# DLRM tower: quarters of a tile through all stages, row scaling moved from VectorE to GpSimd

## The reference

```python
x = layer_norm(dense_t @ Wd.T, gd, bd)                        # 128 wide
y = layer_norm(einsum('bnd,ed->bne', sparse_t, Ws), gs, bs)   # 26 rows x 128
y = layer_norm(einsum('bne,pn->bep', y, Wsi), gsi, bsi)       # 128 x 32
T = concatenate([x[:, None, :], swapaxes(y, 1, 2)], axis=1)   # 33 x 128
Zflat = einsum('bnd,bmd->bnm', T, T)[:, TRIL_I, TRIL_J]       # 528
z = layer_norm(Zflat @ Wl.T, gl, bl)[:, :384]                 # 512, 384 used
h = relu(concatenate([z, r_dense_t], axis=1) @ W_top1 + b_top1)
h = relu(h @ W_top2 + b_top2)
out = h @ W_top3
```

## Time and profile before

| | us |
|---|---|
| median of three runs | 779.56 (778.5 to 780.78) |
| the profiled execution | 779.52 |
| its span, first to last instruction | 777.7 |
| PE matmul busy | 582.8 (75%) |
| DVE busy | 487.4 (63%) |
| POOL busy | 455.2 (59%) |
| ACT busy | 294.0 (38%) |
| mean granted TensorE clock | 0.871 of 2.4 GHz |

### The profile page before, as it was taken

The page is one execution under the profiler, slowest core; times in us unless marked ns, Lnnn a source line. Parts: engine busy times, 40 slices in busy tenths (PEclk is TensorE's granted clock), DMA queues, the critical chain, the costliest instruction groups (busy, mean ns, idle before and its releaser), DMA issues.

```text
span 777.7 us, 18327 instructions
## 1 busy us (share of the span) xinstructions
PE 582.8 (75%) x6783; PEld 476.5 (61%) x6783; DVE 487.4 (63%) x773; ACT 294.0 (38%) x711; POOL 455.2 (59%) x628
## 2 busy tenths in 40 slices
PE   4447556869786987778778888678788887879767
PEld 3334344867675775657667676566667675758555
DVE  4628556559583958467574867458485867768810
ACT  1305533235353534243353334235353434344512
POOL 5666666666666666666666666666666666660000
PEclk9669787779899899998798899879899899999989
DMA  8200011020200202020210202121110202020110
GB/s 305 104 20 21 21 50 38 22 67 21 68 20 22 68 20 67 22 67 22 64 24 22 66 20 67 24 63 25 51 37 22 67 22 67 22 66 6 47 48 1
DMA packets 27200, 36.49 MB, mean 47 GB/s; under 512 B 8917, under 2 KB 17775, under 8 KB 26607
## 3 DMA queue, kind: packets, MB, share of 16 engines
q1 hardware_dynamic: 13808, 21.65, 7.9%
q0 software_dynamic: 13312, 13.66, 7.8%
HBM read 26.09 MB, written 9.18 MB: 45 GB/s over the span
## 4 chain that ended last, share of the span: by engine, by line
POOL 47%; issue 42%; PE 6%; POOLq 1%; DMA 1%; DVE 1%; ACT 1%; SPq 0%; DVEq 0%; ACTq 0%
POOL rows L574 41%; POOL ids L570 6%; PE bank_d L745 2%; PE bank_z L694 1%; PE bank_z L681 1%; POOLq L572 1%; PE bank_z L756 0%; POOLq L573 0%; PE bank_d L716 0%; DMA zx<-zs 0%; DVE y_var L410 0%; DMA rows<-in_table,ids 0%; PE bank_z L763 0%; PE bank_a L716 0%; DMA row_base<-in_row_base 0%
## 5 line engine op out<-in xcount | busy, mean ns | idle before, releaser
L574 POOL DMA_INDIRECT rows<-in_table,ids x416 | 407.0, 978 | 237.7 <-issue 198.8
L681 PE MATMUL bank_z<-r_vec 128*32 128x35 f32 x4096 | 77.6, 204 | 48.1 <-issue 47.3
L681 PEld LDWEIGHTS bank_z<-r_vec 128*32 128x32 f32 x4096 | 58.3, 112 | 71.7 <-issue 67.3
L896 ACT ACTIVATE y_sq<-y 128x512 f32<-128x512 f32 x128 | 75.3, 626 | 66.5 <-DVE y L400 55.8
L379 DVE COPY zs<-bank_z 128x280 f32<-128x280 f32 x32 | 14.4, 450 | 126.2 <-PE bank_z L681 65.9
L694 PE MATMUL bank_z<-wl,zd 128*128 128x512 f32 x160 | 83.2, 639 | 8.4 <-DMA zd<-zx 8.4
L424 DVE TENSOR_TENSOR r_vec<-y,y_r 128x512 f32<-128x512 f32 x128 | 83.3, 692 | 2.2
L912 ACT CAST mixed<-bank_d 64x512 fp32r<-64x512 f32 x64 | 37.1, 580 | 124.4 <-PE bank_d L716 66.0
L729 PE MATMUL bank_b<-mixed,proj_hi 128*128 128x512 f32 x64 | 36.5, 570 | 61.8 <-DVE mixed L388 59.9
L410 DVE TENSOR_REDUCE y_var<-y_sq 128x32 f32<-128x1024 f32 x64 | 77.4, 1210 | 0.7 <-ACT y_sq L896 0.7
L912 ACT CAST mixed<-bank_a 64x512 fp32r<-64x512 f32 x64 | 37.1, 579 | 75.5 <-PE bank_a L716 55.0
(11 more groups left out here) (114 smaller groups left out, 1012.7 us busy)
## 6 DMA issues: line engine op xcount, KB each, us to landing
zx<-zs SPq DMA_DIRECT2D x16, 560.0 KB
rows<-in_table,ids POOLq DMA_INDIRECT x416
dense_t<-in_dense_t SPq DMA_DIRECT2D x1, 2048.0 KB
wl<-in_wl SPq DMA_DIRECT2D x1, 1280.0 KB
w<-in_w SPq DMA_DIRECT2D x1, 1280.0 KB
zd<-zx SPq DMA_DIRECT2D x16, 80.0 KB
wsi_b<-in_wsi_b SPq DMA_DIRECT2D x1, 1248.0 KB
zd<-zx SPq DMA_DIRECT2D x16, 70.0 KB
```

Source lines behind the costliest of these rows:

```text
L574: nc.gpsimd.indirect_dma_start(rows[par][:, c, D * blk:D * (blk + 1)], None, io["table"], bass.IndirectOffsetOnAxis(ap=ids[par][:, n:n + 1 ...
L681: mm = pe.matmul(bank_z[PROJ * s:PROJ * (s + 1), j, n * ITEMS:(n + 1) * ITEMS], own[:, Y0:PAD], own, start=True, stop=True)
L896: nc.scalar.activation(y_sq[:, j % 2, blk, :], y[:, Y_PART[j], blk, :], ACT.Square)\
```

## The change

- The loops over tiles are gone. Every engine's program is written out as 64 quarters k = 4t + q, in stages w = 0 to 73. In one stage the program treats quarter w up to the row factor, quarter w-2 from `mix` to `y_scale`, quarter w-3 in `interact` and `keep_z`; the steps of `linear` and the top layers of older tiles are spread over stages. The steps before `mix` run per quarter; the chunks are grouped 4, 3, 3, 3, so that a quarter's mix needs no later chunk.
- `mix`, `turn`/`gram_product` and `interact` have one PSUM bank each now, `project` two as before. `keep_z` is all on ACT.
- Pool adds all row numbers in one instruction before the first gather. It then issues, for m = 0 to 428, `scale_half(m - 13)` and gather m. `scale_half` multiplies one half chunk (128 by 64) by its factor; this replaces `scale_rows` on DVE. At the first half chunk of each quarter it waits for `rstd_done`, the quarter's row factors.
- Before a gather of tile 2 or later Pool waits for `rows_scaled` of the same half chunk two tiles before.

```diff
-GROUPS = [range(c, min(c + 4, CHUNKS)) for c in range(0, CHUNKS, 4)]
+GROUPS = [range(0, 4), range(4, 7), range(7, 10), range(10, 13)]
+SCALE_LAG = CHUNKS
 # vector
+            for w in range(STAGES):
+                tile, q = divmod(w, BANKS)
+                new, mid = w < QUARTERS, 2 <= w < QUARTERS + 2
+                if new:
+                    square_form(w)
+                    row_mean_square(w)
+                if mid:
+                    keep_low(w - 2, 0)
+                    keep_low(w - 2, 1)
+                if new:
+                    row_reciprocal(w)
+                if mid:
+                    keep_y(w - 2, 0)
+                    keep_y(w - 2, 1)
...
+                if mid:
+                    y_mean_square(w - 2)
+                if q == 0 and 2 <= tile <= TILES + 1:
+                    linear_reciprocal(tile - 2)
+                if mid:
+                    y_reciprocal(w - 2)
+                    y_scale(w - 2, 0)
+                    y_scale(w - 2, 1)
 # gpsimd
+            def scale_half(m):
+                t, n = divmod(m, 2 * CHUNKS)
+                c, blk = divmod(n, 2)
+                q = group_of(c)
+                if n == 2 * GROUPS[q][0]:
+                    pool.wait_ge(rstd_done, BANKS * t + q + 1)
+                    if t:
+                        pool.wait_ge(mix_done, min(BANKS * (t - 1) + q + 2, BANKS * t))
+                half = slice(D * blk, D * (blk + 1))
+                nc.gpsimd.tensor_scalar(scaled[:, c, half], rows[t % 2][:, c, half], row_r[:, n:n + 1], None, ALU.mult)\
+                    .then_inc(rows_scaled, 1)
...
+            for m in range(ROWS_PER_LANE + SCALE_LAG):
+                if m >= SCALE_LAG:
+                    scale_half(m - SCALE_LAG)
+                if m < ROWS_PER_LANE:
...
+                    if t >= 2:
+                        if n == 2 * GROUPS[q][0]:
+                            pool.wait_ge(gathered[t % 2][q], (t // 2) * (32 * len(GROUPS[q])))
+                        pool.wait_ge(rows_scaled, m - 2 * (2 * CHUNKS) + 1)
                     nc.gpsimd.indirect_dma_start(
 # tensor
+            def interact(k):
+                t, q = divmod(k, BANKS)
+                if q == 0:
+                    pe.wait_ge(x_placed, t + 1)
+                if k:
+                    pe.wait_ge(zs_kept, k)
+                pe.wait_ge(r_ready, k + 1)
...
+            for w in range(STAGES + 2):
+                tile, q = divmod(w, BANKS)
+                new, mid, old = w < QUARTERS, 2 <= w < QUARTERS + 2, 3 <= w < QUARTERS + 3
+                if new:
+                    turn(w)
+                if mid:
+                    mix(w - 2)
+                if old:
+                    interact(w - 3)
+                if new:
+                    gram_product(w)
...
+                if 2 <= tile <= TILES + 1 and q == 0:
+                    linear(tile - 2, range(0, STEPS))
+                if mid:
+                    project(w - 2)
```

More of the change, by code:

```diff
@@ L86, in block_rows, with group_of @@
     return PLACES[k][0], PROJ - PLACES[k][1]
+def group_of(c):
+    return next(g for g, chunks in enumerate(GROUPS) if c in chunks)
 WINDOWS, WIN_COLS = chunk_windows()
@@ L225, in tower @@
         stored = sem("stored")
[L227 to L236 removed]
+        bank_y = [bank_b, bank_c]
+        bank_m = bank_a
+        bank_x = [bank_a, bank_d]
+        bank_t = bank_g = bank_z[:, 0, :]
+        bank_i = bank_z[:, 1, :]
+        bank_w = bank_z[:, 2, :]
+        bank_l = bank_z[:, 3, :]
         zx = nc.dram_tensor("zx", (QUAD, PROJ, BLOCKS, QUADS, STEPS), F32, kind="Internal").ap()
@@ new lines, in linear @@
+            def linear(t, steps):
+                if steps[0] == 0:
+                    pe.wait_ge(z_moved, Z_MOVES * (t + 1))
+                    pe.wait_ge(sumx_placed, t + 1)
+                    if t:
+                        pe.wait_ge(z_kept, t)
+                    else:
+                        pe.wait_ge(wl_centred, 1)
+                for s in steps:
+                    mm = pe.matmul(bank_l, zd[:, :, s], wl[:, s, :], start=(s == 0), stop=(s == STEPS - 1))
+                if steps[-1] == STEPS - 1:
+                    mm.then_inc(l_done, 1)
@@ L792, in tile_work @@
-                if top:
-                    first_layer(3)
-                if load:
-                    project(0)
-                if inter:
-                    interact(2)
-                if load:
-                    mix(1)
-                if load and not inter:
-                    fold(range(3, STEPS))
-                if load:
-                    mix(2)
-                if inter:
-                    interact(3)
-                if load:
-                    project(1)
-                    mix(3)
@@ L825, in tile_work @@
-                if more:
-                    turn(t + 1, 1 - par, 2)
-                if load and not inter:
-                    add_up_x(3)
-                if inter:
-                    linear(range(3, STEPS))
-                if more:
-                    turn(t + 1, 1 - par, 3)
-                if inter and not top:
-                    fold_bl()
-                if top:
-                    second_layer()
-                if more:
-                    gram_product(t + 1, 0)
-                    gram_product(t + 1, 1)
```

773 lines of the change are left out of this document (303 added, 470 removed).

## The result

| | before | after |
|---|---|---|
| median of three runs | 779.56 (778.5 to 780.78) | 821.53 (816.28 to 821.88) |
| ratio | | 1.052 [1.045, 1.059] |
| profiled execution, its span | 779.52, 777.7 | 821.88, 819.9 |
| POOL busy | 455.2 (59%) | 643.9 (79%) |
| granted TensorE clock | 0.871 | 0.848 |

The account below looks back on a forecast made before the run. It took Pool as the bound before and DVE and PE taking turns as the bound after: 70 + 46 x 10.75 + 15 x 13.3 - 2 + 47.6 = 810, with 44 for the clock and 1.8 outside the span 856 us (765 to 935).

Parts of the forecast that it names:

- What bounds the kernel before: Kernel before: Pool is bound by its own sequence, 43.6 us a tile; DVE and PE, 63% and 75% busy, have slack.
- Part 1: Pool's sequence after the change: a scaling and gather take 1.57 us (1.46 to 2.1), 40.8 us a tile.
- The gap of 0.81: Pool's idle time behind an addition, 0.81 us; forecast to become 0.30 behind a scaling, with 0.81 kept as the other end.
- the second rival: Pool: a scaling costs as much as an addition did, 2.08 us a pair, 940 us in all; chance 0.10.
- the rival of 0.06: DVE and Pool block one another: each y_scale half waits for a scaling, cycle gains 38 us, 894 us; chance 0.06.
- Part 2: DVE and PE take turns in each stage: 10.75 us, 13.3 with q = 0, 45.6 us a tile, bounding the kernel.
- The first rival: Pool stays the bound and the change is faster: interact's gaps don't appear, stage 9.5 us, 735 us; chance 0.14.
- Part 3: PE's clock: idle times put 40% of certain steps at the lower level, adding 44 us of a possible 110.
- Part 4: Start and end: about 70 us to the first interact, 47.6 at the end; time behind the last gather falls about 14.
- those named as wrong: Profile signs against the forecast: Pool without waits (pair above 1.85 us or stages below 10.2), interact at 1 us, square_form before interact.
- those named as right: Profile signs for it: chain with much DVE, ACT, PE; Pool waiting 2 to 8 us a tile; clock below 0.871.
- the forecast's formula for a Pool-bound kernel: Start, Pool pairs, end and time outside the span: 38.4 + 403 x 1.57 + some 62 + 1.8 gives 735 us.

Follow-up runs that it names:

- experiment 6: Kernel before with one 26-column Pool addition a tile instead of 13 two-column ones, run where the kernel before takes 797.0 to 799.5 us: 1166.83 us, ratio 1.464; again 1.457.
- Experiment 4: Changed kernel with the row scaling back on DVE at the end of each stage, Pool only gathering: 778.62 us, ratio 1.000.
- experiment 3: Changed kernel with y_scale reading its first operand from PSUM instead of the SBUF copy, leaving the bias out: 788.05 us, ratio 1.010.
- 4 (repeated): Changed kernel with row scaling back on DVE, run again where the kernel before takes 797.0 to 799.5 us: 983.2 us, ratio 1.220.
- 5: Changed kernel with row scaling back on DVE and gram_product before interact, where the kernel before takes 797.0 to 799.5 us: 1065.36 us, ratio 1.332; again 1.330.
- 7: Changed kernel without any edit, run where the kernel before takes 797.0 to 799.5 us: 862.27 us, ratio 1.081.

## Why the prediction was right, and where it was not

- **What bounds the kernel before: read from its trace, not tested; its reserve was read wrong.** The one edit of the kernel before, experiment 6, ran in the 798 condition only and made it slower. Experiment 4 takes all scalings and additions in the loop off Pool and reaches the time of before, not more. In the new order the next bound, 43.4 us a tile, lies at Pool's old 43.6.
- **Part 1, Pool's pair: the failed step.** Forecast 1.57 (1.46 to 2.1) and 40.8 a tile, measured 1.67 undisturbed and 1.78 in the mean, 46.3 a tile. Terms: the scaling 0.46, not 0.3 (between the bounds, but I leaned to the 128x2 row, where even one column takes 0.31); the gather 1.01, not 0.96; the gap 0.17, not 0.30. The gap of 0.81 did not stay, so the second rival, a scaling as dear as an addition, is out.
- **Collisions: the rival of 0.06 was real.** Its size, 38 us, was near the 33 that experiment 3 gives back. What I had wrong is who pays: `y_scale` stays at a median of 691 ns, and Pool's gathers and scalings are stretched. My evidence against it was DVE's duration beside gathers, the wrong engine to look at: the row that told it was Pool's addition of 2.02 us.
- **Part 2, the cycle: mechanism shown, one term wrong, and not the bound.** DVE waits for gram behind interact, as forecast (180.6 us in after, 100.7 in experiment 4). The wrong term is interact: 2.0, read from the earlier trace rows, and 0.7 to 0.8 measured. With 0.76 the forecast's own sum is 12.06 + 3 x 9.51 = 40.6 us, and 4 x 0.72 for its clock term makes 43.5; experiment 4 shows 43.4. By quarter the fit is looser: 12.8 against 11.93 measured with q = 0, and 10.2 against 10.24 to 10.72 for the others. The row was no odd one: from its first pass to the end of its last, an interact of before has a median of 1.85 us, and 50 of the 64 have gaps. Wrong was to carry the gaps over to the new program. The first rival named exactly this ("interact's gaps don't appear"), and gave it 0.14 only.
- **Part 3, the clock.** 44 us for 61 stages is 0.72 a stage; it was part of the sum just made and wasn't measured apart. The mean granted clock is 0.848, below 0.871 as forecast; it isn't on the path of after, where Pool sets the pace.
- **Part 4, both ends: right.** First scaling at 39.70 (38.4), Pool idle 18.64 (16), 15 us gained behind the last gather (14), 62.4 us from the end of the last gather to the end of the span (some 62 in the first rival).
- **The signs.** Two of those named as wrong came true: interact below 1 us, and Pool nearly without waits (though its pair was 1.78, not above 1.85, and no quarter's mean was below 10.2). Of those named as right, the chain with much DVE and PE and Pool's waits of 2 to 8 us a tile were absent. Stages of 10.4 to 13.2, a wait of DVE for gram of 180.6/63 = 2.9 us a stage and a clock of 0.848 came, and decided nothing: under a Pool-bound pace, quarters of 8 and 6 gathers make unequal stages too.

With the measured terms the forecast's formula for a Pool-bound kernel gives 39.7 + 403 x 1.78 + 62.4 + 2.0 = 821 us, against 821.9 for the profiled execution (2.0 is the time outside the span). The forecast of 856 was above this because it added too long an interact to the cycle and took too short a scaling for Pool; the first made the cycle the bound and outweighed the second. Both pointed to "slower", and that the time fell within the range is luck as far as the mechanism goes: Pool lost the 42 us, not the cycle.

In the 798 condition the same kernel comes close to what was forecast: 862.3 us, stages of 12.2 in the mean (forecast 12.1), interact 1.63 in the median (2.0), Pool waiting (82.3 - 16.0 - 7.7)/15.5 = 3.8 us a tile, without the start and the end. Not as forecast, its four stages are equally long (12.08 to 12.40, where 14.0 and three of 11.5 were expected). The with their gaps come, however, from an execution of before at 779.5 us, so the gaps are no mark of the 798 condition alone. That kernel runs its tiles in a hardware loop, the changed one is written out; whether that is why they differ in the 779 condition wasn't tried apart.

**What stays open.** Why small matrix passes come in drips and results are released late beside close gathers. Shown is the association. Within one execution of experiments 4 (repeated), 5 and 7 interact has gaps while gathers run and none behind the last one. Between kernels, spacing of 1.25 us without compute on Pool between them costs 1.22 to 1.46 times in the 798 condition and nothing in the 779 one (experiment 4, 1.000), and 1.67 us with a scaling costs 862 against 822. Whether it is how PE's instructions are fetched or how its completions are reported, no run tells apart. The kernel of experiment 4 has the same packets on the queues that its pages mark "instruction" in both conditions (54 with 0.88 MB and 28 with 0.23 MB), so it didn't load more there; how late they came the profile doesn't tell. Nor does any run tell what sets the condition: one chip showed both.

## What to carry to other kernels

Before an operation moves to a bound engine, price it by its fixed part: on Pool 416 small instructions at 0.31 us each outweigh all their columns. Read a collision on the engine that is the bound, not on the one that causes it, and take out the shared memory operand first, since here that alone was worth 33 of 42 us (experiment 3 leaves a bias out for it, so it prices the collision and is no finished kernel). When two stages take turns, measure each alone (one order without the other's work, as in experiment 4) before the sum decides which of two close bounds is the later.

## What the runs showed of the hardware that was not expected

- A Pool `tensor_scalar` is 0.31 us for one column and 0.46 for 64. A gather is 0.94 with a gap of 0.30 behind another gather, and 1.01 with a gap of 0.17 behind a scaling: a scaling adds 1.67 - 1.25 = 0.42 us to the pace, less than its own 0.46.
- A gather, too, takes 1.49 us instead of 1.01 when it starts just after a DVE product of two SBUF operands.
- Removing 12 of 13 small additions a tile, so that gathers follow one another at 1.25 us, made the kernel before 1.46 times as long in the 798 condition. Small work between DMA issues is not always waste.
- The same kernel can stand at 1.000 and at 1.22 times the kernel before in two sets of runs, each with an interval under 1.3% to either side; a single set tells one condition only.
